# An image-row matrix kept per image, with zeros in the rows of the other image

## What is computed

```python
h = concat([tokens(img), txt], axis=1)               # (32, 165, 192)
n = layernorm(h)
q = n @ Wq.T + bq;  k = n @ Wk.T + bk;  v = n @ Wv.T + bv
scores = (q @ k.T) / sqrt(192)
h = h + scores @ v                                    # no softmax in between
```

## Time and profile before

| | |
|---|---|
| median of 3 runs | 1374.36 us (1368.64 to 1376.65) |
| the profiled execution | 1368.88 us |
| its span, first to last instruction | 1367.1 us |
| PE busy | 1236.9 us, 90% |
| DVE busy | 986.1 us, 72% |
| ACT busy | 666.7 us, 49% |
| POOL busy | 411.9 us, 30% |
| mean granted TensorE clock | 0.972 of full speed |

### The profile page before, as it was taken

The page is one execution under the profiler, slowest core; times in us unless marked ns, Lnnn a source line. Parts: engine busy times, 40 slices in busy tenths (PEclk is TensorE's granted clock), DMA queues, the critical chain, the costliest instruction groups (busy, mean ns, idle before and its releaser), DMA issues.

```text
span 1367.1 us, 28240 instructions
## 1 busy us (share of the span) xinstructions
PE 1236.9 (90%) x9938; PEld 1043.0 (76%) x9938; DVE 986.1 (72%) x2685; ACT 666.7 (49%) x1520; POOL 411.9 (30%) x395
## 2 busy tenths in 40 slices
PE   4589999999999999999986899999898999999996
PEld 3367777777677776777765699998787998998995
DVE  3367777777777867778665678777777878888884
ACT  0154555545555455654556555554533444544531
POOL 1111111110111101111010027877776344344344
PEclk7699999999999999999997899999999999999998
DMA  2092211122101222012400333436566666666652
GB/s 92 21 250 59 62 53 40 28 60 60 53 28 39 60 60 53 20 48 60 96 10 9 151 85 73 81 82 176 126 157 159 145 179 155 146 179 154 149 119 30
DMA packets 93596, 123.32 MB, mean 90 GB/s; under 512 B 9152, under 2 KB 85801, under 8 KB 89554
## 3 DMA queue, kind: packets, MB, share of 16 engines
q1 hardware_dynamic: 69090, 100.75, 24.7%
q0 software_dynamic: 24432, 21.62, 11.5%
HBM read 68.94 MB, written 53.38 MB: 89 GB/s over the span
## 4 chain that ended last, share of the span: by engine, by line
PE 59%; DVE 16%; issue 12%; POOL 7%; ACT 3%; another core or an unknown queue 1%; DMA 1%; POOLq 0%; DVEq 0%; SPq 0%; ACTq 0%
PE PS L1486 51%; PE PS L1489 8%; POOL expert_rows L690 3%; POOL rs L624 2%; DVE st L1010 2%; DVE XA L1021 1%; DVE nb L1086 1%; DVE mv L1013 1%; DVE Z L1021 1%; DVE H L1053 1%; ACT XAT L744 1%; POOL out L678 1%; DVE ZS L1068 1%; DVE H L1050 1%
## 5 line engine op out<-in xcount | busy, mean ns | idle before, releaser
L1486 PE MATMUL PS<-w2r,GH 128*120 (+1 forms) x864 | 262.8, 362 | 1.7 <-DVE GL L1255 1.1
L925 ACT ACTIVATE GF<-PS,b1c 128x480 f32<-128x480 f32 x216 | 142.4, 660 | 249.6 <-PE PS L1486 230.0
L624 POOL TENSOR_TENSOR rs<-ve,minus_half 128x3 f32<-128x3 f32 (+1 forms) x80 | 58.8, 736 | 624.6 <-DVE ve L1015 624.6
L728 POOL DMA_INDIRECT out<-YO,ids x100 | 163.0, 1630 | 184.2 <-DVE flag L1439 158.1
L1486 PE MATMUL PS<-w2r,GL 128*120 (+1 forms) x864 | 216.9, 251 | 0.0
L766 ACT ACTIVATE PX<-PS,nb 128x165 f32<-128x165 f32 x576 | 176.9, 413 | 66.2 <-DVE nb L1086 57.7
L1486 PE MATMUL PS<-XH,w1r 128*128 128x480 f32 x432 | 171.7, 398 | 13.3 <-ACT GF L925 8.1
L1486 PEld LDWEIGHTS PS<-w2r,GH 128*120 128x120 f32 x864 | 156.9, 182 | 4.9 <-DVE GL L1255 4.2
L1486 PEld LDWEIGHTS PS<-w2r,GL 128*120 128x120 f32 x864 | 159.1, 184 | 0.0
L1489 PE MATMUL PS<-ident,PX 128*128 128x128 f32 x864 | 138.6, 289 | 19.7 <-DVE PT L1091 11.7
L1086 DVE TENSOR_REDUCE nb<-PS 128x6 f32<-128x990 f32 x96 | 113.4, 1183 | 50.8 <-PE PS L1486 50.4
(11 more groups left out here) (249 smaller groups left out, 2312.4 us busy)
## 6 DMA issues: line engine op xcount, KB each, us to landing
w1r<-expert_w_parts SPq DMA_DIRECT2D x25, 1536.0 KB
expert_rows<-empty SPq DMA_DIRECT2D x45, 369.4 KB, 6.0
RT<-expert_rows SPq DMA_DIRECT2D x25, 369.4 KB
X<-x_scratch SPq DMA_DIRECT2D x11, 360.0 KB, 6.2
out<-X POOLq DMA_DIRECT2D x11, 360.0 KB, 5.7
XP<-in_patches SPq DMA_DIRECT2D x32, 108.0 KB
H<-in_txt SPq DMA_DIRECT2D x16, 192.0 KB, 3.9
out<-H SPq DMA_DIRECT2D x16, 192.0 KB
```

What stands on the lines that cost most here:

```text
L624: nc.gpsimd.tensor_tensor(rs[:, k - 1, 0:n], ve[:, k - 1, 0:n], eps_half[:, 0:n], ALU.pow).then_inc(rstd_ready[k - 1], 1)
L728: nc.gpsimd.indirect_dma_start(out[:, :], bass.IndirectOffsetOnAxis(ap=ids[:, i, t:t + 1], axis=0), YO[:, i % 2, t, :], None, bounds_check ...
L925: nc.scalar.activation(GF[:, m % 3, :], PS[:, 2 + m % 2, 0:GT], ACT.Gelu, bias=bias, scale=1.0).then_inc(gelu_ready, 1)
L1486: return nc.tensor.matmul(o, l, r, start=start, stop=stop)
```

## The change

MI gets a second slot, [P, 2, D] in place of [P, D], and the filler tile `spare` shrinks by as much, so that what lies behind keeps its place. At the start all of MI is set to zero. ScalarE copies the 37 rows of each sequence into that sequence's slot, in two copies instead of one over 128 rows. The rest of each slot stays zero for the whole program. The four MI products (eight passes) take all 128 rows of MI's slot and of VL's tile 2; the rows that belong to the other sequence, or to none, are multiplied by zero. The order of the instructions is as before on every engine, but for the one more copy on ScalarE.

```diff
-    MI = sb(one, "MI", [P, D])
-    sb(one, "spare", [P, 2 * DA + 2 + 4 * DA + 12 * D - 4 * S - 6 * D - 4 * (NIMG + S)])
+    MI = sb(one, "MI", [P, 2, D])
+    sb(one, "spare", [P, 2 * DA + 2 + 4 * DA + 11 * D - 4 * S - 6 * D - 4 * (NIMG + S)])
...
-        nc.gpsimd.memset(MI[:, S:D], 0.0)
+        nc.gpsimd.memset(MI[:, :, :], 0.0)
...
-            copy(MI[:, 0:S], PS[:, 7, 0:S]).then_inc(lin_m_ready, 1)
+            for b in range(2):
+                own = slice(64 * b, 64 * b + NIMG)
+                last = copy(MI[own, b, 0:S], PS[own, 7, 0:S])
+            last.then_inc(lin_m_ready, 1)
...
             mm(o, MT[:, b, q], VL[:, b, :], True, False)
-            mm(o, MI[64 * b:64 * b + NIMG, q], VL[64 * b:64 * b + NIMG, 2, :], False, True)
+            mm(o, MI[:, b, q], VL[:, 2, :], False, True)
...
                 for c in range(2):
-                    own = slice(64 * c, 64 * c + NIMG)
-                    last = mm(image_out[c], MI[own, q], VL[own, 2, :], False, True)
+                    last = mm(image_out[c], MI[:, c, q], VL[:, 2, :], False, True)
```

## The result

The changed kernel takes 1367.37 us (median of 15 runs, 1361.25 to 1369.92), the kernel before, beside it, 1373.51 us (15 runs, 1367.95 to 1378.67). The ratio is 0.9951, with a 95% interval of 0.9931 to 0.997: 0.5% faster, between 0.3% and 0.7%. (The ratio is taken over the single runs and is not exactly the quotient of the two medians; so are the ratios further down.) Forecast were 9.5 us and 0.7%; measured are 6.1 us between the medians and 7.4 us between the spans of the profiled executions (1367.1 and 1359.7). By the number alone the rival "part of the gain is taken up" (6.5 us saved, 1367.9) is nearer than the forecast (1364.9); which of them holds has to be read from the turns.

The account below looks back on a forecast made before the run. PE's order was taken to set the turn. PE's 0.68 us less 0.08 for the copy gives 0.60; 15 x 0.60 plus 0.5 for the first pair is 9.5 us saved, 1364.9 us (0.7% less); range 1358 to 1370.

Parts of the forecast that it names:

- part of the gain is taken up: Rival: transposes behind the products wait for VectorE's or ScalarE's copies, losing 0.2 us a turn; 6.5 us saved, 1367.9; chance 0.08.
- PE's part: PE's image products without pauses: 0.34 us saved at b = 0, 0.19 at b = 1, 0.15 at image queries; 0.68 a turn.
- the pause stays: Rival: MI behind MT pauses for a reason other than its rows; nothing saved, 1375.8 to 1377.4 us; chance 0.04.
- MI's pairs no longer run together: Rival: image-query passes run in a row instead of in pairs, 0.33 us less saved each time; 1370.1 us; chance 0.03.
- the second copy: ScalarE's added MI copy starts 0.21 us after the first, making MT's load 0.08 us late; at worst 0.31 and 0.18.
- all four points: Later places in the turn (two sets of transposes, VectorE's H, PE's 0.34 us wait) that must not hold up the gain.
- H's wait: VectorE waits 0.76 us for PE before H; H can come 0.6 us earlier, leaving a wait near 0.4.
- the wait of 0.34: PE's wait for a copy on VectorE behind H and the statistics; all starts 0.6 us earlier, so the wait stays.
- the two thin margins: Transposes behind b = 0 clear VectorE's copy by 0.07 us; those after the image queries clear ScalarE's by about 0.12.
- the first pair: First pair, before the loop's 15: PE saves some 0.7 us, MT waits 0.21 for the copy; 0.5 saved.
- The low clock: Rival: one more stretch at granted clock 0.50, in the last turns, costs up to 4.9 us; 1369.8 us; chance 0.08.

Follow-up runs that it names:

- two signals: Changed kernel, but each of ScalarE's MI copies signals by itself and sequence 0's products wait only for the first: 1354.58 us, ratio 0.9922 to the kernel before.
- one addition: Kernel with a signal per MI copy, plus both image outputs in one bank, added to H in one VectorE operation: 1357.82 us, ratio 0.987 to the kernel before.

## Why the prediction was right or wrong

**PE's part was right.** 0.68 us in a turn was forecast, and 0.68 was measured as the difference of two kernels that differ in nothing else. That 65 rows count as the full height, which the prediction took from one neighbouring pair of passes with 128 and 65 rows, holds, and the limit lies between 64 and 65. The rivals "the pause stays" and "MI's pairs no longer run together" are out. The weight of the rule in the Trainium skill (TensorE: Matmul & The Clock Gate, The mechanism), that loads overlap a running matmul only where the row groups differ, was judged rightly by the trace: the changed kernel's loads of MI (from 398.32) run beside MT's passes (398.05 to 398.64), on the same rows. One reading behind it was wrong: the row of eight loads "of 128 rows" merges two forms, and four of the eight load 65 rows; the 0.14 us from start to start is the same for both. What the runs show agrees with the Trainium skill (TensorEngine Tiling, Tiling Modes and Key Properties), down to the 64 rows: a pass of 64 rows or 37 between passes of 128 pauses going in and coming out, one of 65 doesn't.

**The term that was mis-sized is the second copy.** "MI's 165 columns take 0.31 where those take 0.33, so I take 0.02 off: 0.21" priced it by two copies that both start on partition 0. Those of the change start on 0 and 64 and stand 0.31 us apart. The delay was 0.18 in place of 0.08, the turn's saving 0.50 in place of 0.60. The bound of 0.18 ("at worst the copies don't overlap at all, 0.31") was in the sum as its far end, and it is what came. The trace before did have a row of a like kind, on another engine: VectorE's two additions for H, 64 rows each, starting on 0 and 64, which last 0.71 us together. The prediction didn't use it.

```profile
405.51 0.71 DVE L1053 TENSOR_TENSOR H<-PS,H 64x192 f32<-64x192 f32 x2
```

**The gain passes through** as said in all four points: H's wait fell to 0.41, the wait of 0.34 stayed, and the two thin margins (0.07 and 0.12 us) held. So the rival "part of the gain is taken up", whose 1367.9 us is near the measured 1367.37, is right about the time and not about the cause.

**The sum.** 15 turns at 0.50 give 7.5 us, and the spans differ by 7.4. That the two are so near is partly luck. From the second pair's first MT product to the last pair's, 14 turns, it is 603.40 us before and 596.41 after, 7.0 us less, as 14 x 0.50 says. The rest of stage one takes 1.4 us less (63.45 and 62.02 us from there to its last product, at granted clocks of 0.84 and 0.83), stage two 1.1 us more (600.4 and 601.5). Nothing of the change is in stage two, and I did not look for the cause. For the first pair I had 0.5; its own part cannot be separated from the start of the program, where the first copy came 0.26 us later in the changed kernel's profile (56.18) than in the one before. The 6.1 us between the medians is below the 7.4 of the spans, but the interval, 0.3% to 0.7%, reaches from 4 to 9.5 us saved and holds both; the forecast's 9.5 us lies at its edge.

**The low clock** was given as a rival with 4.9 us for one more stretch. It has no part in the 0.50 us of a turn, since the turns compared here run at 1.00 in all profiles. Outside the turns it differs from one profile to the next. In the profile before, 39 to 60 us and 60 to 90 us:

```profile
39.00:60.00 21.00, 13.96 (x62) 8.83 (x62) 5.60 (x21) 3.22 (x8) 1.41 (x2) 0.76 0.04 12
60.00:90.00 30.00, 20.04 (x159) 16.31 (x160) 19.97 (x59) 11.60 (x31) 4.81 (x7) 0.77 0.74 188
```

With the copies alone changed:

```profile
39.00:60.00 21.00, 14.22 (x46) 9.53 (x46) 5.12 (x19) 3.50 (x9) 1.42 (x3) 0.54 0.04 12
60.00:90.00 30.00, 21.01 (x121) 15.64 (x125) 14.44 (x48) 8.91 (x24) 2.27 (x3) 0.64 0.52 136
```

At a mean clock of 0.54 and 0.64 PE gets through 54 passes fewer in 51 us. The loop is reached later: the second pair's first MT product starts at 106.15 us, against 99.88 before. But this is not all by which executions differ. From the last pair's first MT product to the end, the profile with two signals takes 654.92 us and the one with one addition 668.87, at mean clocks of 0.97 and 0.96, and the one before 663.86 at 0.97. The kernel before itself has medians of 1366.85 and 1374.16 us in two comparisons that ran on different chips. What makes up these differences is open. A change of 0.1 us in a turn (1.5 us in all) can therefore be read from the turn and not from the medians, and medians are compared only within one comparison.

## What to carry to other kernels

Look for small products between large ones: where one of 64 rows or fewer stands alone among products of more, padding it with zeros to 65 rows or more took away the pauses around it at no cost on PE. Then ask what the padding adds elsewhere: splitting ScalarE's copy into one that begins on partition 0 and one on partition 64 cost its full length once more, so signal each half by itself, or put the split where the next engine has other work. And the same split that the padding brought in may already stand elsewhere on the chain; joining it there was worth nearly as much as the change itself.

## What the runs showed of the hardware

- PE, float32, 192 columns: a product of 64 rows between products of 128 costs 0.33 us a turn more than one of 65, in pauses before and behind it (42.96 and 42.63 us). A product of 65 rows in that place costs as much as one of 128 (42.63 and 42.62 us).
- ScalarE: two neighbouring copies out of PSUM, 165 columns each, start 0.20 us apart when both begin on partition 0, and 0.31 us, their full length, when they begin on 0 and 64. Copies of 192 columns that begin on 0 and 64 start 0.33 us apart, and the first lasts 0.31.
- VectorE: two additions of 64 rows that begin on partitions 0 and 64 last 0.71 us together, one of 128 rows 0.35. Whether the start or only the number of operations makes the difference was not tried.
